# A graph-network, attention and expert kernel on one NeuronCore: two or four 512-column products of constants behind every second step of the gather walk

## The reference, cut to what matters

```python
edge_index = jnp.stack([src, dst])
xn = _layernorm(x, axis=-1)
x = x + _L0_gnn_ref(xn, edge_index, ...) + _L0_mix_ref(xn[None], ...)[0]
x = x + _L0_ffn_ref(_layernorm(x, axis=-1)[None], ...)[0]

# the part of _L0_gnn_ref that the walk computes
neigh_sum = jax.ops.segment_sum(input_matrix[src], dst, num_segments=N_NODES)
deg = jax.ops.segment_sum(jnp.ones_like(dst, ...), dst, num_segments=N_NODES)
neigh_mean = neigh_sum / jnp.maximum(deg, 1.0)[:, None]

# the linear attention: keys are normalised over all nodes, so its second half needs its whole first half
k = jax.nn.softmax(k, axis=-1)
context = jnp.einsum('bhdn,bhen->bhde', k, v)
out = jnp.einsum('bhde,bhdn->bhen', context, q)
```

## Time and profile before

| | |
|---|---|
| median of the three runs | 2311.33 us |
| the profiled execution: time, span | 2314.33 us, 2311.9 us |
| mean granted clock of TensorE | 0.816 of full |
| the walk, first to last addition of DVE | 131 to 1393 us |
| busy share of the whole span: PE, DVE, POOL, ACT | 72%, 58%, 53%, 34% |
| gathers of the walk | 832 |

### The profile page before, as it was taken

The page is one execution under the profiler, slowest core; times in us unless marked ns, Lnnn a source line. Parts: engine busy times, 40 slices in busy tenths (PEclk is TensorE's granted clock), DMA queues, the critical chain, the costliest instruction groups (busy, mean ns, idle before and its releaser), DMA issues. The chain is left out here.

```text
span 2311.9 us, 34640 instructions
## 1 busy us (share of the span) xinstructions
PE 1657.1 (72%) x9290; PEld 1316.8 (57%) x9291; DVE 1345.5 (58%) x3663; ACT 796.7 (34%) x1603; POOL 1218.3 (53%) x1204
## 2 busy tenths in 40 slices
PE   2846666666556566788666763441999999999997
PEld 2634343434335344434434443441999999999996
DVE  7844343434334466677766667652666666666663
ACT  0200000000001133232433335650666666666663
POOL 4466666666666566666666652664233333333333
PEclk8967767677777778799887775555999999999999
DMA  7833333333333266665666645756465555555554
GB/s 212 280 112 99 101 98 103 99 105 103 100 103 87 87 219 201 189 192 175 199 200 198 189 126 162 252 192 157 97 136 131 131 132 128 135 130 133 130 130 91
DMA packets 207237, 337.79 MB, mean 146 GB/s; under 512 B 34085, under 2 KB 151354, under 8 KB 206119
## 3 DMA queue, kind: packets, MB, share of 16 engines
q0 software_dynamic: 78912, 205.54, 34.1%
q1 hardware_dynamic: 118592, 128.08, 17.7%
q10 hardware_dynamic: 9638, 3.13, 0.6%
HBM read 250.75 MB, written 86.68 MB: 146 GB/s over the span
## 5 line engine op out<-in xcount | busy, mean ns | idle before, releaser
L1180 DVE TENSOR_TENSOR acc_lent<-acc_lent,bank 128x258 f32 x832 | 350.3, 421 | 517.4 <-remote 226.1
L651 POOL DMA_INDIRECT G<-z_d,edge_tabs_lent x416 | 407.3, 979 | 263.4 <-issue 115.2
L651 POOL DMA_INDIRECT w2s_lent<-z_d,edge_tabs_lent x416 | 411.0, 988 | 187.5 <-issue 117.7
L1597 PE MATMUL bank<-w2s_lent 128*128 128x258 f32 x832 | 319.0, 508 | 211.9 <-issue 111.6
L1597 PEld LDWEIGHTS bank<-w2s_lent 128*128 128x128 f32 x832 | 179.8, 244 | 324.3 <-issue 209.5
L1597 PE MATMUL bank<-G,S_lent 128*128 128x258 f32 x832 | 269.2, 448 | 118.2 <-issue 51.8
L691 POOL DMA_INDIRECT out_dram<-G,acc_lent x112 | 180.5, 1612 | 208.3 <-DVE G L1486 129.8
L1465 DVE TENSOR_TENSOR acc<-w1s,acc 128x512 fp32r<-128x512 f32 x224 | 154.9, 693 | 214.4 <-ACT acc L914 195.2
L1597 PEld LDWEIGHTS bank<-G,S_lent 128*128 128x128 f32 x832 | 161.5, 217 | 202.2 <-issue 148.9
L1783 PE MATMUL bank<-w2s,acc 128*128 x896 | 262.2, 293 | 1.6 <-DMA edge_tabs<-w2lo_d 1.6
L1760 PE MATMUL bank<-acc 128*128 128x256 f32 x896 | 258.0, 288 | 5.0 <-DVE acc L1473 5.0
(11 more groups left out here) (274 smaller groups left out, 3040.2 us busy)
## 6 DMA issues: line engine op xcount, KB each, us to landing
S<-w2lo_d POOLq DMA_DIRECT2D x56, 512.0 KB
edge_tabs<-w2lo_d POOLq DMA_DIRECT2D x56, 512.0 KB
acc_lent<-bucket_d SPq DMA_DIRECT2D x56, 266.0 KB, 3.0
xTs<-xnT_d SPq DMA_DIRECT2D x98, 128.0 KB
bu_d<-w2s_lent SPq DMA_DIRECT2D x98, 128.0 KB
w2s_lent<-bu_d SPq DMA_DIRECT2D x12, 768.0 KB
w1s<-in_L_ffn_W_dram SPq DMA_DIRECT2D x8, 1024.0 KB
w2s_lent<-in_L_ffn_W_dram SPq DMA_DIRECT2D x32, 256.0 KB
```

The source lines that it names most:

```text
L651: pool.indirect_dma_start(out=G_half[half][:, k, 0:D], out_offset=None, in_=z_d[:, :], in_offset=bass.IndirectOffsetOnAxis(ap=srcT[:, step ...
L1180: dve.tensor_tensor(to, to, bank[k % 4][:, 0:ACCW], ALU.add).then_inc(s["acc_done"], 1)
L1597: pe.matmul(bank[k % 4][:, 0:ACCW], S_half[half][:, k // S_GROUP, k % S_GROUP, :], G_half[half][:, k, :], start=True, stop=True).then_inc( ...
```

## The change

The `follow` calls inside `walk` go away (behind steps 3, 5, 7 and behind the other work at steps 3 and 7). In their place a new function `keep_busy` runs behind steps 1, 3, 5 and 7 of every block, after the other work that hangs on the step. It issues four bfloat16 products of the same constants, each 512 columns wide (128 columns read four times), in blocks 0 to 53, and two of them in blocks 54 to 103. They write bank 7 and carry no wait and no semaphore. The `follow` calls outside `walk` stay. No other engine's instructions change.

```diff
@@ -365,6 +365,7 @@
         UN = 8
+        MIXED = NT + 5
@@ -1585,6 +1586,12 @@
+            def keep_busy(n):
+
+                for _ in range(n):
+                    pe.matmul(bank[7][:, :], before[:, :], ones_b[:, :].rearrange("p (o n) -> p o n", o=1).to_broadcast([P, 4, P]),
+                              start=True, stop=True)
+
             def walk(i, half, turn, hooks={}):
@@ -1595,12 +1602,10 @@
                     pe.matmul(bank[k % 4][:, 0:ACCW], S_half[half]..., G_half[half]..., start=True, stop=True).then_inc(s["p_ready"], 1)
-                    if k in (3, 5, 7):
-                        follow()
                     if k in hooks:
                         hooks[k]()
-                        if k in (3, 7):
-                            follow()
+                    if k in (1, 3, 5, 7):
+                        keep_busy(4 if i < MIXED else 2)
```

## The result

The changed kernel takes 2338.36 us (median of 12 runs, 2319.28 to 2344.20) beside 2315.93 us of the kernel before on the same chip (12 runs). The ratio is **1.0079, 95% interval 1.0058 to 1.0100**: 0.8% slower, where I had forecast 4% faster. It lies within my own bound for "same", 1%, but the interval leaves out 1. The profiled execution took 2342.45 us. Lines of the walk have moved by one or a few: the step's product is now L1604, its addition L1181, the gather L652, the constant product L1592.

What follows compares the result with a forecast made beforehand. POOL's gathers were taken as the floor, with POOL held back by TensorE's late reports. Terms -72 - 10 - 18 = -100 against 2314.33 us gave 2214, predicted as 2210 us for the median; 8-in-10 range 2150 to 2330.

Steps and rivals of the forecast that it cites:

- POOL's pace as the floor: Walk: POOL issues all gathers one after the other, 1.26 us a step, so no block beats 10.1 us.
- Price of a wide product: Walk: a constant product of 512 columns costs TensorE 0.22 to 0.23 us at full clock.
- The clock follows: First part: a TensorE 80% busy keeps its full clock; granted clock over 0.9, from 0.71 and 0.73.
- What is left idle is 2 us a block ... if reports are then late by less than DVE's spare time, POOL's own pace is the bound: First part: filled TensorE idles only for gathers; with reports under 5.3 us a block late, blocks fall from 11.6 to 10.1.
- -72: First part: reaching POOL's pace takes 1.5 us from each of 48 blocks, 72 us in all.
- -10: After the first part: POOL runs on behind the keys' maximum and `M2`; 10 us saved, bounds 0 to 20.
- -18: Mixing part: half the folding blocks' filling saves 0.45 us in each of 41 blocks; bounds 0 to -74.
- The ring term: Two chains after the first part find the 16-step ring not full, so POOL runs on; 10 us saved.
- The folding blocks as the experiment already made: Mixing part: eight expert-folding blocks, 3.4 us more products each, clock 0.94, showed filling removes 1.0 us of waiting a block.
- The bounds beside the forecast: Whole kernel: 2185 to 2245 us around the forecast of 2210, said to follow from the second and third term's bounds.
- C: Rival, walk: work behind a step does not cure late reports; idle time merely filled, 2311 us within 1%; chance 0.12.
- D: Rival, first part: clock does not stay up, TensorE becomes the bound; +82 us, 2395, at clock 0.6; chance 0.18.

Runs made afterwards that it cites:

- six: Changed kernel with half as many wide products again (six in the first part, three in the mixing part); 0.9991 of the kernel before.
- no_fill_again: Changed kernel without any constant product inside the walk, run in another session; 0.9978 of the kernel before, which took 2102.48 us there.
- after_again: The changed kernel unaltered, timed again on another chip; 1.0030 of the kernel before, which took 2102.48 us there.
- twice_e: Changed kernel with twice the wide products (eight and four), on a chip where the kernel before took 2324.38 us; 2360.30 us, 1.0159.
- before_same: The kernel before, word for word, on another chip; 0.9978 of the kernel before's 2317.11 us there.
- const_bf16_b: Changed kernel with each step's float32 product replaced by a bf16 product of constants; 2299.80 us against the kernel before's 2308.96, 0.9969.
- twice: Changed kernel with twice the wide products (eight in the first part, four in the mixing part); 1.0363 of the kernel before's 2102.48 us.
- const_bf16: Changed kernel with each step's float32 product replaced by a bf16 product of constants; 2099.81 us against the kernel before's 2105.77, 0.9981.
- no_fill: Changed kernel without any constant product, narrow or wide, inside the walk; 0.9988 of the kernel before's 2106.47 us.

## Why the prediction was wrong

The sizes, step by step:

- *POOL's pace as the floor*: 10.1 us a block forecast; 10.3 to 10.4 in free sessions (495.6 us for 48 blocks with six, 497.2 with no_fill_again). Right. So was the size of what could be won: the first 48 blocks take 577.0 us before, and 80 us less in a free session with no fill at all.
- *Price of a wide product*: 0.22 us forecast; 0.86 from the start of four to what follows them (270.42 to 271.28). Right.
- *The clock follows*: over 0.9 forecast, 0.90 and 0.88 measured, 1.00 in a free session. Nearly right, and worth nothing: the kernel is 0.5% slower at 1.00 (after_again, 1.0030) than at 0.83 (no_fill_again, 0.9978). The granted clock of the earlier trace rows cost nothing that could be won in this way.
- ***"What is left idle is 2 us a block ... if reports are then late by less than DVE's spare time, POOL's own pace is the bound"*: the step that failed.** All of the -72, -10 and -18 stand on it. I took TensorE's idle time beside a late report for a part of its cause, a pair that "wait for each other". Late reports sum to 266.4 us after 267.6, and to 238.7 with TensorE 95% busy (twice_e). The ring term gave nothing either: blocks 48 to 53 take 81.8 us after 82.2. The mixing part lost 17 us where 18 were to be won.
- *The folding blocks as the experiment already made*: in that trace they do have fewer late reports, 11.1 us in eight blocks, 1.4 a block, against 2.4 in the 16 ahead (37.7) and 1.8 in the 24 behind (42.9). In the changed kernel it is 2.3, 2.4 and 2.3 (18.1, 38.8 and 55.8 us): the 16 blocks that were filled as I wanted, from 37.7 to 38.8, gained nothing. The other held traces differ (1.7 against 2.2 and 2.2 a block in before_same, 2.7 against 2.2 and 1.9 in const_bf16_b), so eight blocks were too few to read an effect of filling from them.
- *The bounds beside the forecast*: "2185 to 2245 by the bounds of the second and third term" does not follow from these terms. Their bounds (0 to -20, 0 to -74) give 2145 to 2239; the stated lower bound is a narrower guess.

Of the rivals C, "the reports are late for a reason that work behind them does not cure", is what happened, down to its mark (waits of 4 us, TensorE idle beside them at full clock), and I gave it 0.12. Its price of zero left out the added work. That can be sized roughly over the kernels of the held sessions, each against the kernel before in its own. The change adds 1264 products of 0.22 us and takes out the narrow ones, 250 us net, and costs 0.8% of 2316, 18 us; twice adds another 274 us of TensorE, 0.8% again; const_bf16_b takes 270 us out of the steps (0.11 us from one to the next instead of 0.43, 832 times) and gives back 1.1%, 25 us. So where reports are late, **7 to 9% of TensorE's time comes through to the end**, an estimate from one held session for each kernel whose intervals leave it between about 3 and 12%. A product ahead of a step delays it now and then, in the 13 us more of products not there in the first part. D's mechanism, TensorE as the bound, exists, but it takes twice the products, and it shows in free sessions alone (3.5 to 3.8%); D's clock did not fall.

The evidence was there before. The example of the earlier trace rows shows steps and `kv` behind the late report, and the earlier trace rows four long products behind another. A theory that says "idle first, report late after" has to be checked on the order in time, and in both places the report was due before TensorE stopped.

**What stays open** is what makes reports late in some sessions. It is not the program (three kernels were traced in both kinds of session, and their first 48 blocks have 4.0 to 4.7 us of late reports in the one and 239 to 273 in the other), not the chip as such (chip 5 has both), not idle time or the clock, not the step's float32 product or its gathered operands. It may lie in what else uses the chip or in which of its cores runs the kernel; the runs name neither. The rival that stands nearest is the profiler itself: every run compared here has its span and clock, so it was on in all of them, and the held traces are the ones in which half of the semaphore updates have no record. Whether the kernel has two times with the profiler off was not tested. no_fill has the lowest time in free sessions, 0.9974 to 0.9988 of before and below the changed kernel; in a held session it was never run.

## What to carry to other kernels

Before an idle engine is filled, look in the order of time whether the idle time begins before or after the event that is late; if after, it is a consequence and filling it adds work to a path that does not need it. A granted clock below one is a cost only if the engine is what others wait for by name and its products are not there; sort the waits into "product not over" and "over, but not reported" before anything is priced. And when a forecast rests on a stall of unnamed origin, run the unchanged kernel again elsewhere first, and count whether the trace has a record of every semaphore update: here the first alone moved the time by ten times what the change did, and the second tells the two kinds of trace apart.

## What the runs showed of the hardware

- The same program, with the same instructions, takes 2102 to 2106 us in some sessions and 2309 to 2324 in others, 10%, in seven and four of eleven. The difference is steady within a session and can change on one chip within four minutes. Most of it lies in the walk: of the 202 us between the traces of const_bf16 and const_bf16_b, 27 lie between the walk's end and the last output, and the first 48 blocks alone have 78.
- In the held traces the semaphore updates have a record in half of the cases (16,333 in const_bf16_b, 33,559 in const_bf16). TensorE's reports reach DVE up to 15.6 us after the product's modelled end, DVE's reach TensorE 0.05 to 0.06 us after the addition's.
- Late reports are released at distances near multiples of 0.71 us, whatever the products are. In the first 48 blocks of the five held traces, 75 to 97% of the distances under 8 us between additions that waited over 0.8 us and came over 0.8 us late lie within a tenth of a period of a multiple of 0.711 us, where chance would give 20%. DVE's additions after waits in const_bf16_b:

```profile
336.97 0.42 DVE L1181 TENSOR_TENSOR acc_lent<-acc_lent,bank 128x258 f32 x1 [1.65 <-PE bank L1604]
339.08 0.42 DVE L1181 TENSOR_TENSOR acc_lent<-acc_lent,bank 128x258 f32 x1 [1.69 <-PE bank L1604]
...
342.63 0.42 DVE L1181 TENSOR_TENSOR acc_lent<-acc_lent,bank 128x258 f32 x1 [2.52 <-issue]
344.04 0.42 DVE L1181 TENSOR_TENSOR acc_lent<-acc_lent,bank 128x258 f32 x1 [0.99 <-PE bank L1604]
348.27 0.42 DVE L1181 TENSOR_TENSOR acc_lent<-acc_lent,bank 128x258 f32 x1 [3.81 <-remote]
349.72 0.42 DVE L1181 TENSOR_TENSOR acc_lent<-acc_lent,bank 128x258 f32 x1 [1.03 <-PE bank L1604]
```

  The starts are 2.11, 3.55, 1.41, 4.23 and 1.45 us apart, which is 3, 5, 2, 6 and 2 times 0.70 to 0.73. The rows of the changed kernel above, 269.70 to 281.13, give 1.41, 5.02, 2.15 and 2.85: 2, 7, 3 and 4 times. It looks as if something with a period of about 0.7 us lets reports through; no run here says what.
